# Second experts of a two-layer transformer kernel: the next block's rows are transposed and copied earlier in the block loop

## The reference

```python
def _L1_ffn_ref(x, Wg, bg, W1, b1, W2, b2):
    B, T, C, E, K, H = (4, 128, 128, 8, 2, 512)
    xf = x.reshape(N, Cx)
    gate = xf @ Wg + bg
    topv, topi = jax.lax.top_k(gate, K)
    probs = jax.nn.softmax(topv, axis=-1)
    comb = jnp.zeros((N, E)).at[jnp.arange(N)[:, None], topi].set(probs)
    h = jax.nn.relu(jnp.einsum('nc,ecf->nef', xf, W1) + b1)
    y = jnp.einsum('nef,efc->nec', h, W2) + b2
    return jnp.einsum('nec,ne->nc', y, comb)
```

## Time and profile before

| what | us |
|---|---|
| median of 3 runs | 1866.24 (1857.8 to 1871.12) |
| profiled execution, its own time | 1866.84 |
| its span in the trace | 1865.1 |
| first copy of the block loop to the last | 1519.8 to 1795.0 |

### The profile page before, as it was taken

One profiled execution on the slowest core, in us unless ns is written; L12 is line 12 of the kernel. 1 busy time (PEld: TensorE's weight loads), 2 busy tenths in 40 slices (PEclk: granted clock), 3 DMA queues, 4 the chain that ended last, 5 costly groups with the idle time before them and its releaser, 6 DMA issues.

```text
span 1865.1 us, 37875 instructions
## 1 busy us (share of the span) xinstructions
PE 1576.1 (85%) x12583; PEld 771.1 (41%) x12583; DVE 1276.2 (68%) x3279; ACT 1163.8 (62%) x1878; POOL 903.4 (48%) x1691
## 2 busy tenths in 40 slices
PE   5799999999959999699999999999997238888860
PEld 3333444444323444234444444444443126655640
DVE  7566777777657888747766777766766626666647
ACT  3777787787748899545566555556554526666640
POOL 6244544544412333434434458566476535555555
PEclk9889999999979999879999999999989569999995
DMA  5221122122119910122221222222221222222218
GB/s 152 79 38 36 35 38 44 35 38 44 35 46 356 386 49 1 46 46 52 41 46 35 51 47 67 57 56 50 51 65 53 99 96 75 79 73 70 79 57 263
DMA packets 234308, 142.95 MB, mean 77 GB/s; under 512 B 183875, under 2 KB 201283, under 8 KB 233093
## 3 DMA queue, kind: packets, MB, share of 16 engines
q1 hardware_dynamic: 222464, 120.67, 24.8%
q0 software_dynamic: 9088, 18.89, 3.1%
q10 hardware_dynamic: 2564, 0.97, 0.2%
HBM read 38.61 MB, written 59.90 MB: 53 GB/s over the span
## 4 chain that ended last, share of the span: by engine, by line
PE 41%; DVE 11%; issue 6%; ACT 4%; POOL 3%; another core or an unknown queue 2%; DVEq 1%; DMA 1%; POOLq 1%; SPq 0%; ACTq 0%
PE OP L2130 8%; PE M L2093 5%; PE OP L1995 5%; PE SP L1975 4%; DVE mx L1325 4%; PE SP L2289 4%; PE SP L2110 2%; PE M L2068 2%; ACT vs L960 2%; PE M L2089 2%; PE M L2084 2%; POOL h_dram L490 2%; PE OP L2304 2%; ACT pt L959 1%
## 5 line engine op out<-in xcount | busy, mean ns | idle before, releaser
L861 ACT ACTIVATE pt<-SP 128x768 f32<-128x768 f32 x256 | 207.4, 810 | 253.2 <-PE SP L2110 237.0
L1325 DVE TENSOR_REDUCE mx<-M 128x2 f32<-128x512 f32 (+1 forms) x384 | 257.9, 683 | 108.7 <-PE M L2093 97.5
L529 POOL TENSOR_SCALAR_AFFINE_SELECT pt<-pt 128x256 f32<-128x256 f32 x512 | 199.7, 415 | 266.4 <-ACT pt L861 264.5
L748 ACT ACTIVATE pt<-SP 128x1024 f32<-128x1024 f32 x256 | 255.6, 1020 | 76.3 <-PE SP L1865 76.1
L560 POOL DMA_INDIRECT y_dram<-hT,dest x156 | 158.7, 1018 | 147.5 <-DVE hT L1618 111.4
L959 ACT ACTIVATE pt<-SP,b 128x512 f16<-128x512 f32 x156 | 108.1, 693 | 133.5 <-PE SP L2289 80.5
L1884 PE MATMUL OP<-pt,vs 128*32 128x256 f32 x1408 | 188.4, 390 | 0.0
L490 POOL DMA_INDIRECT h_dram<-hT,slot x128 | 130.4, 1018 | 57.3 <-issue 31.6
L1612 DVE TENSOR_TENSOR pt<-vs,pt 128x512 f16<-128x512 f32 x156 | 107.2, 691 | 72.5 <-ACT vs L960 50.8
L2130 PE MATMUL OP<-pt,vs 128*32 128x128 f32 (+1 forms) x1408 | 152.9, 340 | 4.6 <-POOL pt L529 4.6
L2289 PE MATMUL SP<-ksT,shared 128*128 128x512 f16 x468 | 122.5, 385 | 36.9 <-DVE ksT L1591 29.0
(11 more groups left out here) (324 smaller groups left out, 3303.1 us busy)
## 6 DMA issues: line engine op xcount, KB each, us to landing
h_dram<-shared SPq DMA_DIRECT2D x8, 4488.0 KB, 33.7
hT<-h_dram SPq DMA_DIRECT2D x39, 264.0 KB
rows<-g_dram SPq DMA_DIRECT2D x4, 2048.0 KB, 7.4
pt<-y_dram SPq DMA_DIRECT2D x32, 256.0 KB, 3.5
x_sb<-in_x SPq DMA_DIRECT2D x8, 512.0 KB, 9.1
pt<-in_w SPq DMA_DIRECT2D x4, 1024.0 KB
out<-x_sb SPq DMA_DIRECT2D x16, 256.0 KB, 3.0
y_dram<-hT,dest POOLq DMA_INDIRECT x156
```

What stands on the lines that cost most here:

```text
L529: last = pool.affine_select(out=diag, in_=diag, compare_op=ALU.is_ge, fill=0.0, base=0, pattern=[[0, 2], [1, P]], channel_multiplier=-1)
L748: act.activation(pt[:, u % 4], SP[u % 2][:], ACT.Exp, scale=SCALE).then_inc(s["exp"], 1)
L861: act.activation(pt[:, u % 4, :, 0:384], SP[u % 2][:, :, 0:384], ACT.Exp, scale=SCALE).then_inc(s["exp"], 1)
L1325: dve.tensor_reduce(to, M[:, k % 2, :].rearrange("p (j k) -> p j k", j=4 if k < 4 else 2), AX.X, ALU.max).then_inc(s["mred"], 1)
```

## The change

TensorE transposes the rows of the next block right behind hidden 1 instead of behind outputs 1, and VectorE copies them behind low 0 instead of behind low 2. No instruction is added or taken away, and no wait is changed.

```diff
@@ VectorE, blocks()
                 for g in range(NBLK):
                     targets(g)
                     low(g, 0)
+                    if g + 1 < NBLK:
+                        take(g + 1)
                     low(g, 1)
                     low(g, 2)
-                    if g + 1 < NBLK:
-                        take(g + 1)
                     low(g, 3)
                     if g:
                         leave(g - 1)
```

## The result

The changed kernel takes 1855.32 us (median of 20 runs), the kernel before 1874.26 in the same session (runs of both kernels on one chip): a ratio of 0.9922, 95% interval 0.9893 to 0.9952. That is 0.78% of 1874, some 15 us; the two medians by themselves lie 18.9 us apart. I had forecast 29 us. The direction and the range (1824 to 1866) held, the size did not: it came out at about half by the ratio, at two thirds by the medians.

A forecast was written before the change was run, and what follows sets the result against it. The loop was taken as bound by scatter group, y seen 6.0 later, leave 0.69 and 0.28. Pitches of 6.95, 6.95 and 5.55 average 6.48 against 7.24: 38 x 0.76 = 29 us off 1866.8, so 1838; range 1824 to 1866.

The forecast's parts named there:

- The wait for the copy goes fully: TensorE's wait before hidden 0 for VectorE's copy, 1.56 us in the loop worked through, vanishes with the earlier copy.
- VectorE catches up, the load is in time: nothing: VectorE's lows 1 and 2 come at most 0.6 us later and recover; the earlier-needed row load also costs nothing.
- The hold: During GpSimd's scatter group, others see TensorE's results 1.8 to 2.8 us late; y seen at 6.0 gives a 6.97 us loop.
- TensorE's sum is unchanged: TensorE's work stays 6.15 us a loop; y ends earlier in successive scatter groups, mean loop 6.48 instead of 7.24.
- the 4.0: Time after a scatter group's start when y is seen if it ends below 2.2 us into the group.
- the groups of 5.55: Scatter groups 5.55 us apart when low 3 sets the end; one to every two of 6.95, mean 6.48.
- y is never seen before 6.0: Rival: hold lasts to the group's end, only the leave's wait behind low 3 goes; 6.95 a loop, 11 us, 1855; chance 0.22.
- p: Place of the end of y within its scatter group, in us after the group's start; 3.2 before the change.
- The products themselves are late: Rival: TensorE's recorded ends are computed, so it is full and its idle time only moves; 1866 us; chance 0.10.
- Joined holds: Rival, slower: the next scatter group's hold begins before the last ends, adding 5.5 us; 1873 to 1907 us; chance 0.10.
- the stated 8.95 and 1627.2: Chain sums: next hidden 0 at earliest 8.95 us after a scatter group's start; next group at 1627.2 when low 3 decides.

The follow-up runs named there:

- the third run: Changed kernel, unaltered, run once more against the kernel before on the chip of the session without the hold: 1862.25 us, ratio 0.9951, loop 7.00.
- the second profile: Changed kernel, unaltered, in another session against the kernel before: 1868.07 us, ratio 0.9998, loop 7.09.
- split: Scatter in two pairs, second after next block's y, against the kernel before: changed order 1847.86 and 1851.84 us (0.9852, 0.9896); order before 1877.16 us (1.0041).

## Why the prediction was half right, by its own steps

- *The wait for the copy goes fully.* Right: from 28 times to one. The copy starts at 1673.73, 1.7 us ahead of the hidden 0 of 1675.40.
- *VectorE catches up, the load is in time: nothing.* Right. Neither shows as a wait in the rows above, and without the scatter the changed order runs at TensorE's own 6.14.
- *The hold sets the loop, not the wait.* Right, and the runs without the scatter show it: 6.16 and 6.06, with the order almost without effect. The cycle of group, y seen, leave 0.69, 0.28, next group stands in the changed kernel as it was worked out, 6.80 against 6.95, since y is seen at 5.83 instead of 6.0. (In the other two profiles of the changed kernel it is seen at 5.9.) What follows, too: the leave waits for y itself now, in 32 loops, and seldom for its turn behind a low.
- *TensorE's sum is unchanged, 6.15 a loop, so y's end moves 0.8 earlier in each group, until it falls below 2.2 and is seen at 4.0.* **This is the step that failed, in both of its halves.** The first: y ends at 1675.56, 2.97 after its group's start, and ends 2.97 into the next group too (1680.86 + 1.50 − 1679.39). TensorE runs through its own work only until the hold stops it: 0.50 at 1678.28, 0.94 at 1685.05. Its loop is 6.15 plus that stop and settles at the groups' distance, 6.80 in the rows shown where the sum had a mean of 6.48. I took the lateness for one of news alone. The second half is wrong by itself: where y did end below 2.2, in the other two profiles, it was seen at 5.1 to 5.8 and not at 4.0, as in the rows of 1.80 and 5.78. I had put the 4.0 together from the transposes and hidden 3 of two loops, and y did not follow them. So without TensorE's stops, too, the groups of 5.55, which bring the mean from 6.95 to 6.48, could hardly have come.
- Why the rows of the kernel before didn't warn of the stop is open. TensorE stood for the copy there, until 4.22 into the group of 1614.68, then ran through 5.7 without a break. It may be that an engine that has just stood gets further in a hold; no run tests that.
- So the rival *y is never seen before 6.0* came true (chance 0.22): groups at an even distance, 11 us, and 15 to 17 measured. That its 1855 is the measured 1855 is luck, since it was counted from 1866 and the kernel before took 1874 beside the changed one. It did not name TensorE's stop. The argument against it, that p must then fall to 1.35, where things are seen earlier, failed by the same two halves. The 16.8 us of the profiled stretch lie between its 11 and my 29; the ratio gives 15, the other two sessions 0 and 9.
- *The products themselves are late.* I set 0.13 us of one early row against it. Half of it is true: TensorE does stop in a hold. But it had time to give, since the loop got shorter, and it starts 14 matmuls behind y's last one while y isn't seen.
- *Joined holds.* Not seen in the profiled run, but there in the other two, though rarely: after groups 6.1 apart TensorE was stopped several times, and three loops of 9.26 to 9.98 us stand among those of mostly 6.6 to 7.6. In others hidden 3 was the product held to the end (it ended 2.28 into the group of 1619.23 in the third run, and its relu started at 5.85), so that low 3 and the leave behind it came late. Groups 8.7 us or more apart come up six times in the second profile, four times in the third and never in the first. This is a good part of why the change was worth less there.
- *The sums.* The relu pair with what lies before the low takes 1622.19 − 1620.84 = 1.35, not 1.26. With 1.35 the chains do give the stated 8.95 and 1627.2; with the 1.26 that stands there they give 8.86 and 1627.1. It changes nothing that failed.

What stays open: what the scatter takes from TensorE, whether it is GpSimd's issuing or the transfers, why the hold was absent in one session, and why TensorE's half alone costs 1%.

## What to carry to other kernels

When an engine goes on at a fixed distance from another engine's event, whatever it was doing, look for a hold and ask whether it stops the engine or only hides its results; an instruction run that is cut in two under "issue" tells the first. A wait that lies inside such a hold is worth little until the hold is shortened: here order and split gave 0 to 0.8% and −0.4% alone, and 1.0 to 1.5% together. Before a rule is drawn from two or three rows ("what ends early is seen early"), look for it in the other loops of the trace and with the very product that the sum turns on. And take the kernel before in each session: it moved by 2.7% between sessions, more than the order or the split did.

## What the runs showed of the hardware

- With four indirect DMAs of 128 rows each from GpSimd in a row, y is seen 2.3 to 3.4 us after its end in the profile of the changed kernel wherever VectorE waits for it, and up to 4.0 in the third; without the hold a relu starts 0.14 after its product. TensorE stops, in the loops shown 4.6 to 5.2 us after the first of the four began, and goes on at 5.66 to 5.78 (three kernels, other instructions each time). With two in a row ScalarE sees a product 1.10 us late at most, in one execution; with plain writes from SyncE's queue there is none.
- A later scatter brings the news of y sooner and moves the stop into the middle of its product, so the stop isn't tied to an instruction or a wait of the program.
- When y ends only 1.80 us into such a run of four, it is still seen at 5.78.
- The hold is not there in every session: the kernel before took 1824.07 us in one and 1867 to 1874 in five others, one of them on the same chip.
